# Four cross-attention layers on one core: the first stage regrouped from one chunk to two

## What is computed

```python
def _cross_attention(q_in, kv_in, wq, bq, wk, bk, wv, bv, wo, bo, bias_k, bias_v):
    qh = (q_in @ wq + bq).reshape(b, q_len, H, K)
    kh = (kv_in @ wk + bk).reshape(b, t, H, K)
    vh = (kv_in @ wv + bv).reshape(b, t, H, K)
    kh = jnp.concatenate([kh, jnp.broadcast_to(bias_k, (b, 1, H, K))], axis=1)
    vh = jnp.concatenate([vh, jnp.broadcast_to(bias_v, (b, 1, H, K))], axis=1)
    logits = jnp.einsum('bqhk,bthk->bhqt', qh, kh) / scale
    weights = jax.nn.softmax(logits, axis=-1)
    ctx = jnp.einsum('bhqt,bthk->bqhk', weights, vh).reshape(b, q_len, H * K)
    return ctx @ wo + bo
...
h = _layer_norm(x, ln1_scale, ln1_offset)
x = res + _cross_attention(h, xf_1, wq1, ...)
h = _layer_norm(x, ln2_scale, ln2_offset)
x = res + _cross_attention(h, xf_2, wq2, ...)
```

## Time and profile before

| what | value |
|---|---|
| runs | 1552.82, 1553.26, 1553.35 us |
| span of the profiled execution, first to last instruction | 1550.8 us |
| time of the runs beyond that span (1553.26 - 1550.8) | 2.5 us |
| matmuls busy | 1517.9 us, 98% |
| VectorE busy | 974.2 us, 63% |
| ScalarE busy | 855.8 us, 55% |
| GpSimd busy | 402.3 us, 26% |
| granted TensorE clock, mean | 0.996 |

### The profile page before, as it was taken

How to read it: one execution, slowest core, us unless ns; L and a number is a source line. 1 busy time by engine, 2 the same in 40 slices (tenths; PEclk the granted TensorE clock), 3 DMA queues, 4 the chain that set the end, 5 groups by cost and what they waited for, 6 DMA issues and landing times. The chain is left out here.

```text
span 1550.8 us, 41283 instructions
## 1 busy us (share of the span) xinstructions
PE 1517.9 (98%) x17264; PEld 1304.4 (84%) x17264; DVE 974.2 (63%) x2115; ACT 855.8 (55%) x1610; POOL 402.3 (26%) x422
## 2 busy tenths in 40 slices
PE   8999999999999999999999999999999999999996
PEld 7888888888888888888888888978878988888864
DVE  7755555555577555555555576479996558865366
ACT  5553453453455453443443566576777567765476
POOL 1231011011033011101201123036764206542052
PEclk9999999999999999999999999999999999999998
DMA  6010010010010010010100000020002000000001
GB/s 229 2 70 2 29 43 1 29 42 1 29 42 2 29 42 1 29 43 1 31 27 29 28 2 28 1 84 2 3 29 83 1 28 3 31 2 28 8 22 55
DMA packets 17688, 46.20 MB, mean 30 GB/s; under 512 B 1344, under 2 KB 11600, under 8 KB 14560
## 3 DMA queue, kind: packets, MB, share of 16 engines
q1 hardware_dynamic: 13312, 39.33, 7.4%
q10 hardware_dynamic: 4192, 4.24, 0.8%
HBM read 39.37 MB, written 4.19 MB: 28 GB/s over the span
## 5 line engine op out<-in xcount | busy, mean ns | idle before, releaser
L175 PE MATMUL ps<-ch,W 128*128 128x512 f32 (+1 forms) x2484 | 596.5, 386 | 1.4 <-ACT arena L1725 0.6
L175 PEld LDWEIGHTS ps<-ch,W 128*128 128x128 f32 x2484 | 432.6, 188 | 87.5 <-issue 2.2
L175 PEld LDWEIGHTS ps<-W,split_arena 128*128 128x128 f32 x3084 | 392.6, 188 | 25.7 <-issue 4.2
L175 PE MATMUL ps<-W,split_arena 128*128 128x256 f32 x3084 | 406.5, 283 | 3.5 <-DVE split_arena L1226 2.4
L175 PE MATMUL ps<-W,ch 128*128 128x512 f32 (+1 forms) x864 | 203.5, 384 | 0.3
L892 ACT ACTIVATE arena<-ps 64x256 f32<-64x256 f32 x256 | 97.0, 379 | 187.8 <-PE ps L791 184.8
L991 DVE TENSOR_REDUCE small<-ps 128x4 f32<-128x260 f32 x128 | 54.1, 422 | 221.1 <-PE ps L720 221.0
L175 PEld LDWEIGHTS ps<-W,ch 128*128 128x128 f32 x864 | 151.6, 188 | 28.4 <-ACT arena L1713 0.9
L952 ACT ACTIVATE arena<-ps,hbias 128x512 f32<-128x512 f32 x128 | 87.8, 688 | 119.2 <-PE ps L175 118.3
L1226 DVE TENSOR_TENSOR split_arena<-arena,split_arena 128x512 fp32r<-128x512 f32 x96 | 71.9, 749 | 125.4 <-ACT split_arena L1258 113.8
L930 ACT ACTIVATE arena<-arena 128x260 f32<-128x260 f32 x128 | 54.3, 425 | 142.0 <-DVE arena L994 142.0
(11 more groups left out here) (168 smaller groups left out, 1967.7 us busy)
## 6 DMA issues: line engine op xcount, KB each, us to landing
raw<-wpack SPq DMA_DIRECT2D x23, 1028.0 KB, 4.9
arena<-vb_in SPq DMA_DIRECT2D x8, 512.0 KB, 5.8
x_sb<-x_in SPq DMA_DIRECT2D x4, 512.0 KB, 9.6
arena<-ctxT SPq DMA_DIRECT2D x4, 512.0 KB, 9.9
spill<-x_sb ACTq DMA_DIRECT2D x1, 2048.0 KB, 11.4
arena<-spill ACTq DMA_DIRECT2D x1, 2048.0 KB, 8.3
arena<-ctx_tok SPq DMA_DIRECT2D x16, 128.0 KB, 2.1
out<-x_sb SPq DMA_DIRECT2D x7, 256.0 KB, 2.5
```

Source lines behind the costliest of these rows:

```text
L175: last = e.matmul(dst, lhs[a], rhs[b], start=start and n == 0, stop=stop and n == 2, skip_group_check=True)
```

## The change

Steps are done two at a time. With a = 2d and b = 2d+1, block d of the new `pe_attend` is: (values of the two steps before, where their pair is even,) keys of a and b, out of a-4 and b-4, transposes of a-2 and b-2, queries of a and b, then the **visit**: heads of a-2 and b-2, scores of a and b. Buffers for keys, queries, exponentials, transposed weights and split heads are doubled; `keys_bank` and its fellows give the banks, and each of them now has two or three users in a block. Out runs two steps later than before. The first two blocks, the two blocks at the turn from the first to the second cross-attention (16 and 17) and the last four steps (60 to 63, one at a time) have orders of their own. Values come after the visit instead of around the transposes.

```diff
+        def pe_visit(e, d):
+            a, b = 2 * d, 2 * d + 1
+            e.wait_ge(a_qe, two(a, 1))
+            pe_heads(e, a - 2)
+            wait(e, a_acc, two(b - 4, 1))
+            pe_heads(e, b - 2)
+            pe_scores(e, a)
+            pe_scores(e, b)
...
+        def pe_upper(e, d):
+            a, b = 2 * d, 2 * d + 1
+            behind = values_behind(d - 1)
+            if behind:
+                pe_values_behind(e, d - 1)
+            for h in range(2):
+                if behind:
+                    e.wait_ge(a_ve, values_done(a - 2, h))
+                e.wait_ge(a_sub, two(a - 2, h))
+                pe_key(e, a, h)
+            for h in range(2):
+                if behind:
+                    e.wait_ge(a_ve, values_done(b - 2, h))
+                e.wait_ge(a_ol, two(a - 4, 1))
+                pe_key(e, b, h)
...
+            e.wait_ge(a_sub, two(b - 2, 1))
+            pe_out(e, a - 4)
...
+            pe_out(e, b - 4)
+            for i in range(2):
+                e.wait_ge(a_ke, two(a, i))
+                pe_transpose(e, a - 2 + i)
...
+        def pe_block_second(e):
+            for h in range(2):
+                e.wait_ge(a_sub, two(0, h))
+                pe_key(e, 2, h)
...
+        def dve_softmax(e, d):
+            a, b = 2 * d, 2 * d + 1
+            dve_shifts(e, a - 2)
...
+            if d != TURN + 2:
+                dve_heads(e, a - 4)
+            dve_shifts(e, b - 2)
+            if d != TURN + 2:
+                dve_heads(e, b - 4)
+            dve_scale(e, a - 2)
```

```diff
+            projections_read(e, n - 2)
+            for wide in (slice(0, PACK // 2), quarter(3))[:2 - b]:
+                ins = e.tensor_copy(W[b][0][:, wide], raw[:, wide])
...
+            a = quarter(2)
             pack_read(e, n - 2)
...
+            e.tensor_copy(W[b][0][:, a], raw[:, a]).then_inc(p_out, 1)
+            e.wait_ge(p_out, nth + 1)
+            e.tensor_tensor(W[b][1][:, a], raw[:, a], W[b][0][:, a].bitcast(F32), ALU.subtract).then_inc(w_lo.sem, 1)
```

More of the change, by code:

```diff
@@ L666, in key_slots, with heads_free @@
+        def heads_free(e, t):
+            wait(e, a_wo, two(t - 1 if t >= SINGLE + 2 else t - 2, 1))
         def key_slots(h):
@@ L683, in pack_ready, with norm_out, pe_norm @@
                 e.wait_ge(w_lo.sem, w_lo.at(t // NCH))
[L685 to L701, removed]
-                    wait(e, a_ol, two(t - 1, 1))
-                else:
-                    e.wait_ge(a_sub, two(t, 1))
-                norm0.pe(e, n[1], norm_bank(n[0]), n[0])
-        def pe_scores(e, t):
-            n = norm_turn(t - 1, 1, 2)
-            if t == 0 or n is not None:
-                l, c = n or (0, 0)
-                e.wait_ge(norm0.s["ev"].sem, norm0.s["ev"].at((l * NCH + c) * KT + KT - 1))
-            e.wait_ge(a_kb, t // NCH + 1)
-            e.wait_ge(a_ve, values_done(t, TPC - 1))
+        def norm_out(e, l, c):
+            e.wait_ge(norm0.s["ev"].sem, norm0.s["ev"].at((l * NCH + c) * KT + KT - 1))
+        def pe_norm(e, l, c):
+            b = norm_banks(l, c)
+            norm0.pe(e, c, (b, b + 1), l)
+        def pe_scores(e, t):
+            if t % NCH == 0:
+                e.wait_ge(a_kb, t // NCH + 1)
             for h in range(2):
@@ L964, in act_last_probs @@
+            act_exp(e, SINGLE + 3)
+            e.activation(spare, col("one"), ACT.Gelu)
+            e.wait_ge(a_q, two(STEPS - 1, 1))
+            piece_act(e, NPAIR + 1, 2, 0)
         def act_last_probs(e):
@@ L1030, in dve_stats, with dve_mean, dve_bias_keys @@
             norm0.dve_stats(e, c, l)
+        def dve_mean(e, l, c):
+            norm0.dve_newton(e, c, l)
+            e.scalar_tensor_tensor(nmean, mv[:, :, 0], -1.0, rstd, ALU.mult, ALU.mult).then_inc(second_mean, 1)
+        def dve_bias_keys(e, u):
+            bias_ready(e, u)
+            wait(e, a_S, two(u - 1, 1))
+            for p in range(2):
+                for h in range(2):
+                    at = 0 if h == 0 else SEQ
+                    ins = e.tensor_copy(ks[p][h][:, :, at:at + 1], each(head_col(u, 2, h), BPC))
+            ins.then_inc(a_kb, 1)
@@ new lines, in dve_attend @@
+            dve_scale(e, 0)
+            dve_scale(e, 1)
+            norm0.dve_lo(e, 3)
+            for k in range(F_PIECES - 1):
+                second_dve(e, k)
+            for d in range(2, SINGLE // 2):
+                if d == TURN:
+                    dve_block_turn(e)
+                elif d == TURN + 1:
+                    dve_block_after(e)
+                else:
+                    dve_block(e, d)
+            dve_softmax(e, SINGLE // 2)
+            dve_bias_keys(e, SINGLE)
+            dve_add(e, SINGLE - 4)
```

791 lines of the change are left out of this document (550 added, 241 removed).

## The result

The kernel with the change takes 1559.9 us (median; 1559.0 to 1562.2), the kernel before 1553.1 measured beside it: ratio 1.0045, 95% interval 1.0031 to 1.0059. The forecast was 1545.4, faster. The profiled execution has a span of 1557.3 us against 1550.8, 6.5 us more.

The account below looks back on a forecast made before the run. It took TensorE's own pace as the bound in the steady part, with VectorE nearly as full at the start. Terms -18.2 + 6.3 + 1.5 + 2.5 = -7.9 took 1553.3 to 1545.4 us, range 1539 to 1552.

Parts of the forecast that it names:

- term 1: Visits to heads and scores: 0.51 us of changing over each, 30 fewer visits, 15.3 us less.
- term 2: Matmuls slower behind a change or transposes: some 60 such tails go, between nothing and 4.2 us, taken as 3.2 less.
- Does the rest keep up in a block?: Whether VectorE, ScalarE and the weights keep up with TensorE inside a block: they do, cost 0.
- rival C: Slower: keys of b wait for the heads' remainder in all 14 odd blocks of full price; 1556.6 us, chance 0.07.
- Rival B: Visits cost the same however grouped, so only half of term 1 and term 2 comes: 1554.7 us, chance 0.09.
- Term 3: The start: VectorE's order leaves TensorE idle 8.1 us in place of 1.8, cost 6.3 us.
- Term 4: The clock: the 4.8 us pause at the start may halve it, costing between 0 and 2.4 us, taken as 1.5.
- Term 5: The turn, blocks 16 and 17: waits for norms and value copies cost 2.5 us, with bounds of 0 and 6.

Follow-up runs that it names:

- run 1: The changed kernel plus 16 dummy identity matmuls in TensorE's pause at the head of the second block: 1555.9 us, ratio to before 1.0020.
- run 8: The version with run 5's orders and run 6's later weights, with VectorE's and TensorE's order at the start changed once more: 1553.4 us, ratio to before 0.9998.
- run 6: The changed kernel with the weight transfers of odd pairs started after the visit's last scores: 1557.2 us; with run 5's orders as well, 1553.7 us.
- run 2: The changed kernel with the heads done by one matmul of 64x128 weights in place of two of 64x64: 1605.2 us, ratio 1.033.
- run 3: The changed kernel with the start reordered: first shifts before chunk 3's context, queries of chunk 2 before the transposes: 1556.1 us.
- run 7: The version with run 5's orders and run 6's later weights, plus eight identity matmuls in each of two TensorE pauses at the start: 1551.7 us, ratio 0.9988.
- run 4: The changed kernel with waits and VectorE's copies reordered at the turn (blocks 16 and 17): 1557.8 us.
- run 5: The changed kernel with the reorderings of run 3 and run 4, plus ScalarE reorderings at the start and first single block: 1555.8 us, ratio 1.0016.

## Why the prediction was wrong

It left out one cost as large as its whole result, and under-sized another.

- **Terms 1 and 2** were right wherever TensorE was not kept waiting. In undisturbed blocks the visits at 423.98 and 445.85 us are 21.87 apart (forecast 21.9; two such steps took 22.49 before), and the heads pair takes 2.03 as worked out from the earlier trace rows. With values in it a block takes 32.75 where two steps took 33.44. So a block gains 0.62 to 0.69 us, where term 1 alone would give 0.51: term 2 is there too. With the 18.2 us of the forecast the account below closes to 0.3 us.
- **"Does the rest keep up in a block?"** asked this of VectorE, ScalarE and the weights, and there the answer 0 was right: no keys waited for heads' remainders (rival C falls). It did not ask it of TensorE's own instruction supply. **That is the step that failed**, a cost put at nothing: term 1 took the pace of 52 heads in a short visit for the pace of any length. The cover was there in the trace before: a visit of 192 instructions in 2.2 us, with large matmuls behind it, ended before a late packet mattered (from 40 to 898 us no gap at one of the 256-instruction places was over 0.34 us, against 0.23 for a large matmul). Without that cover the stalls are 9.1 us in the profiled execution. Rival B named the instruction stream, but as an even price of each visit; in fact a visit is mostly either free or loses some 0.4 us and more.
- **Term 3**, 8.1 us of idle time at the start: the gaps are 1.49, 0.27, 0.11, 5.46 and 0.79, sum 8.1. The sum is right, partly by luck: I had 1.75 at the keys of step 1, where 0.27 was, and had missed that queries of step 0 wait 1.49 for the values' copies. The pause for the first shift was 5.46 against 4.8.
- **Term 4**, the clock: 1.5 forecast, 1.7 measured (run 1 shows it). The page of the Trainium skill that I had weighed here, "TensorE: Matmul & The Clock Gate", Why this matters for your kernels, was right in direction: the clock fell 2.0 us into the pause. The size was between the two ends, and not the full 2.4 that I had set beside the page.
- **Term 5**, the turn, was sized too small: 2.5 forecast, 6.0 measured, the upper bound. The idle stretches are 2.18, 0.12, 1.60 and 0.89 against 0.54 before, 4.3 more. The largest was read wrongly: norm (1, 1) waits for a count that VectorE raises in the order a, a, b, b, a, a, so that "two values of b" also stand behind work I had put later. And the second fall of the clock, 3.4 us at half pace and so 1.7, was not thought of, since I looked for it in the start alone.
- The single blocks at the end of the stage lost 1.3 (heads of step 58 behind ScalarE's probabilities), which no term had.

Together: -18.2 + 6.3 + 1.7 + 6.0 + 1.3 + 9.1 = +6.2, against +6.5 between the spans. The sign itself hangs on the fetch: by this sum the change without it would have been 3 us faster, not 8.

## What to carry to other kernels

Small matmuls packed into one long stretch save the changeovers (0.5 us each here), but ask first whether their instructions arrive: count matmuls and weight loads per microsecond and compare the stretch with a packet of 256. When a change leaves every named wait in place and some repeated block is longer at irregular places, look for "issue" in the waits and for instruction packets in the DMA view. "issue" alone proves nothing: the 1.45 us under that name at 44 us went in run 8, when VectorE made the normed tiles earlier. Count the instructions up to each stall instead, and see whether the counts differ by multiples of 256. A variant that adds a few idle-time instructions ahead of the stretch then tells fetch from work in one run.

## What the runs showed that I had not expected

- TensorE's instruction supply has fixed places, 256 instructions apart, at which a dense stretch can stop. At 95 instructions a microsecond it stopped each time such a place lay 2.66 to 3.71 us into a stretch of 384. The stall ended 2.2 to 2.9 us after the start of the instruction packet that lay in the visit.
- A transfer of data beside such a stretch makes the packet 0.4 to 0.6 us later (run 6) and the stall longer.
- The executions with stalls scatter: 1552.5 to 1554.3 for the kernel before in 15 runs, 1548.9 to 1552.8 for the fastest variant in 11. Whether the fetch makes the scatter is not shown, since run 2, which has no such stall, runs from 1603.1 to 1607.0 in 4.
- With two columns of tiles side by side 128 matmuls of 64x64 weights take 2.03 us, and 64 matmuls of 64x128 weights, the same products, take 3.72.
- The clock's fall is not a matter of one pause's length alone. A pause of 2.18 or 2.19 us at 472 to 477 us was followed by a fall in the changed kernel and in runs 3 and 6, and by none in run 1 (granted clock 1.00 from 477.0 to 480.7). One of 2.23 to 2.28 us near 515 us was followed by a fall in runs 7 and 8, and by none in runs 4 and 5. Why was not found.
